# Feed-forward loop in fp32: paired bn_stats, half of the tanh additions on VectorE, gn and the statistics one step sooner

## The reference, cut to what matters

```python
def step(h, _):
    h = h + 0.01 * jnp.tanh(h)
    h = h * jax.nn.sigmoid(h)
    h = _layernorm(h, ln_w, ln_b)          # mean and variance over 64 features, eps 1e-5
    h = jnp.einsum('bsc,dc->bsd', h, W) + b
    return (h, None)
x, _ = jax.lax.scan(step, x, None, length=N_ITERS)    # N_ITERS = 30
...
h = h + _L0_ffn_ref(_layernorm(h, axis=-1), ...)      # 64 x 96 rows of 64 features
```

## Time and profile before

| what | us |
|---|---|
| runs shown | 2052.88, 2053.17, 2066.5 |
| median | 2053.17 |
| profiled execution, its own time | 2048.48 |
| its span | 2046.7 |
| TensorE, VectorE, ScalarE, GpSimd busy in the span | 1798.6, 1523.3, 1233.2, 861.9 |

### The profile page before, as it was taken

The page is one execution under the profiler, slowest core; times in us unless marked ns, Lnnn a source line. Parts: engine busy times, 40 slices in busy tenths (PEclk is TensorE's granted clock), DMA queues, the critical chain, the costliest instruction groups (busy, mean ns, idle before and its releaser), DMA issues. The chain is left out here.

```text
span 2046.7 us, 73424 instructions
## 1 busy us (share of the span) xinstructions
PE 1798.6 (88%) x25670; PEld 1546.0 (76%) x25701; DVE 1523.3 (74%) x4623; ACT 1233.2 (60%) x2911; POOL 861.9 (42%) x841
## 2 busy tenths in 40 slices
PE   2401299999999999999999999999958899999998
PEld 2401299999999999999999999999948477777776
DVE  3201188888888888888888888888857888888887
ACT  0100277777777777777777777777715466666665
POOL 5000123233332323232332323232214899999997
PEclk9999999999999999999999999999979899999999
DMA  3332200000000000000000000000022000000000
GB/s 116 75 74 60 61 18 19 17 19 17 19 17 17 19 17 19 17 19 17 19 17 17 18 17 19 17 19 17 13 57 62 1 0 0 0 0 0 0 0 31
DMA packets 60784, 48.85 MB, mean 24 GB/s; under 512 B 18368, under 2 KB 58108, under 8 KB 59772
## 3 DMA queue, kind: packets, MB, share of 16 engines
q1 hardware_dynamic: 58790, 47.72, 8.7%
q10 hardware_dynamic: 1972, 0.86, 0.2%
HBM read 19.92 MB, written 8.93 MB: 14 GB/s over the span
## 5 line engine op out<-in xcount | busy, mean ns | idle before, releaser
L681 POOL TENSOR_TENSOR y0lo<-y_whole,y0hi 125x384 f16<-125x384 f32 x410 | 376.2, 918 | 1048.0 <-ACT y_whole L639 1048.0
L643 ACT ACTIVATE z1hi<-ps 128x375 f16<-128x375 f32 x820 | 398.5, 486 | 341.2 <-PE ps L582 341.2
L706 DVE TENSOR_TENSOR z1lo<-ps,z1hi 128x375 f16<-128x375 f32 x820 | 449.8, 549 | 192.3 <-ACT z1hi L643 192.3
L581 PE MATMUL ps<-ATlo,y0hi 125*128 125x150 f16 x2460 | 584.6, 238 | 0.0
L580 PE MATMUL ps<-AThi,y0hi 125*128 125x150 f16 x2460 | 566.6, 241 | 2.0 <-POOL y0lo L681 2.0
L582 PE MATMUL ps<-AThi,y0lo 125*128 125x150 f16 x2460 | 564.5, 239 | 0.0
L711 DVE TENSOR_TENSOR y<-ps,negb 125x384 f32<-125x384 f32 x820 | 451.1, 550 | 29.6 <-PE ps L597 0.7
L595 PE MATMUL ps<-W1hi,z1hi 128*128 128x128 f16 x2460 | 459.3, 221 | 0.2 <-DVE y L711 0.2
L597 PE MATMUL ps<-W1hi,z1lo 128*128 128x128 f16 x2460 | 453.5, 219 | 0.0
L596 PE MATMUL ps<-W1lo,z1hi 128*128 128x128 f16 x2460 | 453.2, 219 | 0.0
L635 ACT ACTIVATE y0hi<-ps 125x384 f16<-125x384 f32 x820 | 404.8, 494 | 77.2 <-PE ps L560 77.2
(11 more groups left out here) (197 smaller groups left out, 2360.4 us busy)
## 6 DMA issues: line engine op xcount, KB each, us to landing
z_static<-zk SPq DMA_DIRECT2D x205, 93.8 KB, 1.9
pooled_rows<-stage SPq DMA_DIRECT2D x820, 2.5 KB
zk<-z_parts SPq DMA_DIRECT2D x16, 360.4 KB
xs<-in_x_v SPq DMA_DIRECT2D x3, 1201.2 KB
xs<-in_x_v SPq DMA_DIRECT2D x5, 720.7 KB
z_parts<-zp SPq DMA_DIRECT2D x20, 180.2 KB
parts<-pooled_rows SPq DMA_DIRECT2D x8, 256.0 KB, 6.1
h_rows<-h SPq DMA_DIRECT2D x16, 96.0 KB, 1.8
```

Of the source, the lines that this page charges most:

```text
L581: nc.tensor.matmul(o, hi, alo, start=False, stop=False, skip_group_check=True)
L643: nc.scalar.activation(z1hi[:, q, 0:GV], ps[:, Z1B + q % 2, 0:GV], ACT.Identity).then_inc(z1hi_done, 1)
L681: nc.gpsimd.tensor_tensor(y0lo[0:R, par, q, :], y0f[0:R, q, :], y0hi[0:R, par, q, :], ALU.subtract).then_inc(y0lo_by_pool, 1)
L706: nc.vector.tensor_tensor(z1lo[:, q, 0:GV], ps[:, Z1B + q % 2, 0:GV], z1hi[:, q, 0:GV], ALU.subtract).then_inc(z1lo_done, 1)
```

## The change

- **Statistics.** A bn_stats now reads two rows of 64 in alternation (`rearrange("p i d -> p d i")`): its even elements are one row, its odd elements the other. So its two triples are the whole statistics of two rows, and four bn_stats of 128 elements serve a chunk. `dm`, `s`, `q`, `sm` and the addition on GpSimd go; one `tensor_scalar` (L1338, 128x8) adds 64 eps to the squared parts and writes `var`. GpSimd keeps the power alone. In the first iteration the centring takes the mean straight from the pair (L1349).
- **Tanh addition.** Even chunks keep the matmul. For odd chunks VectorE does it in PSUM with one scalar_tensor_tensor (L1366), behind a wait for `th`. `y_ready` becomes two semaphores, one for each kind.
- **Order.** Lags: statistics and pow 2 to 1, gn 4 to 3, T 4 to 3; gT stays at 4 and the weights at 5. TensorE issues the addition ahead of the transposes; VectorE issues the odd addition first in its body.

```diff
         bs, bs0 = (sb(f"bn_pairs{i}", [P, 2, CP, 6]) for i in range(2))
...
                 def body(s, c, on, half):
-                    if on(2):
-                        n, b = s - 2, c % 2
-                        pool.wait_ge(parts_done, 2 * n + 2)
+                    if on(1):
+                        n, b = s - 1, (c - 1) % 2
+                        pool.wait_ge(var_done, n + 1)
                         if late(n, 2):
                             pool.wait_ge(gn_done, n - 1)
-                        inverse_roots(s2, q2, var, rs, b, n, var_done, rs_done)
+                        nc.gpsimd.tensor_tensor(rs[:, b, :], var[:, b, :], expo[:], ALU.pow).then_inc(rs_done, 1)
...
+                    if on(0) and c % 2 == 0:
+                        pe.wait_ge(th_done, s + 1)
+                        nc.tensor.matmul(ps[:, c, :], pct[:], th[:, c % 2, :], start=False, stop=True,
+                                         skip_group_check=True).then_inc(y_ready[0], 1)
-                    if on(4):
-                        n, b = s - 4, c % 2
+                    if on(3):
+                        n, b = s - 3, (c - 3) % 2
                         pe.wait_ge(gn_done, n + 1)
...
+                def statistics(src, pairs, var, b, n, bns, made):
+
+                    for j in range(CP):
+                        last = v_.bn_stats(pairs[:, b, j, :], src[:, 2 * j:2 * j + 2, :].rearrange("p i d -> p d i"))
+                    last.then_inc(bns, 1)
                     dve.wait_ge(bns, n + 1)
...
+                    v_.tensor_scalar(var[:, b, :], squares(pairs, b), D * EPS, None, ALU.add).then_inc(made, 1)
...
+                def body(s, c, on, half):
+                    if on(0) and c % 2 == 1:
+                        dve.wait_ge(th_done, s + 1)
+                        v_.scalar_tensor_tensor(ps[:, c, :], th[:, c % 2, :], 0.01, ps[:, c, :],
+                                                ALU.mult, ALU.add).then_inc(y_ready[1], 1)
+                    if on(3):
+                        n, cn, b = s - 3, (c - 3) % CH, (c - 3) % 2
                         dve.wait_ge(rs_done, n + 1)
```

More of the change, by code:

```diff
@@ L1196, in feed_forward @@
         gT = sb("gT", [P, 2, CP * P])
[L1198 to L1203, removed]
+        bs, bs0 = (sb(f"bn_pairs{i}", [P, 2, CP, 6]) for i in range(2))
         var, var0 = (sb(f"var64_{i}", [P, 2, CR]) for i in range(2))
@@ L1237, in steps, with squares, means @@
                     before(s)
-                body(s, s, lambda lag, s=s: s - lag >= 0)
+                body(s, s, lambda lag, s=s: s - lag >= 0, lambda lag, s=s: (s - lag) // 2)
             with eng.Fori(1, ITERS) as it:
                 for c in range(CH):
-                    body(it * CH + c, c, lambda lag: True)
+                    body(it * CH + c, c, lambda lag: True, lambda lag, c=c: it * (CH // 2) + (c - lag) // 2)
             for s in range(N, N + LAG):
-                body(s, s - N, lambda lag, s=s: 0 <= s - lag < N)
+                body(s, s - N, lambda lag, s=s: 0 <= s - lag < N, lambda lag, s=s: (s - lag) // 2)
         def late(n, k):
             return not isinstance(n, int) or n >= k
+        def squares(pairs, b):
+            return pairs[:, b].rearrange("p j (i k) -> p (j i) k", i=2)[:, :, 2]
+        def means(pairs, b):
+            return pairs[:, b].rearrange("p j (i k) -> p (j i) k", i=2)[:, :, 1]
         out_rows = out.rearrange("b s d -> (b s d)").rearrange("(c p n) -> c p n", c=CH, p=P)
@@ L1262, in _ @@
                 pool.wait_ge(expo_made, 1)
[L1264 to L1268, removed]
                 def first(c):
                     if c < CH:
[L1272 removed]
+                        pool.wait_ge(var0_done, c + 1)
                         if c >= 2:
                             pool.wait_ge(x0_ready, c - 1)
[L1275 removed]
+                        nc.gpsimd.tensor_tensor(rs0[:, c % 2, :], var0[:, c % 2, :], expo[:], ALU.pow).then_inc(rs0_done, 1)
                 first(0)
[L1278 to L1281 removed]
+                def body(s, c, on, half):
+                    if on(1):
+                        n, b = s - 1, (c - 1) % 2
+                        pool.wait_ge(var_done, n + 1)
                         if late(n, 2):
                             pool.wait_ge(gn_done, n - 1)
[L1284 removed]
+                        nc.gpsimd.tensor_tensor(rs[:, b, :], var[:, b, :], expo[:], ALU.pow).then_inc(rs_done, 1)
                 steps(pool, body, lambda s: first(s + 1))
@@ L1290, in _, with body @@
                 nc.scalar.activation(warm[:], ident[:, 0:1], ACT.Silu)
-                def body(s, c, on):
+                def body(s, c, on, half):
                     if on(0):
@@ L1295, in body @@
                         if late(s, 2):
-                            act.wait_ge(y_ready, s - 1)
+                            act.wait_ge(y_ready[c % 2], half(2) + 1)
                         nc.scalar.activation(th[:, c % 2, :], ps[:, c, :], ACT.Tanh).then_inc(th_done, 1)
@@ L1299, in body @@
                         n, cn = s - 1, (c - 1) % CH
-                        act.wait_ge(y_ready, n + 1)
+                        act.wait_ge(y_ready[cn % 2], half(1) + 1)
                         if late(n, NG):
@@ L1337, in body @@
                         last.then_inc(gT_ready, 1)
[L1338 to L1341, removed]
                 steps(pe, body, first)
@@ L1357, in centre @@
                 def centre(c):
                     b = c % 2
+                    rows = h2[:, c, :].rearrange("p (r d) -> p r d", d=D)
                     dve.wait_ge(h2_loaded, (c + 1) * 16)
                     if c >= 2:
[L1362 to L1371, removed]
+                        dve.wait_ge(rs0_done, c - 1)
@@ L1373, in first @@
+                        dve.wait_ge(centred, c - 1)
+                    statistics(rows, bs0, var0, b, c, bn0, var0_done)
+                    v_.tensor_tensor(x0c[:, b, :].rearrange("p (r d) -> p r d", d=D), rows,
+                                     spread(means(bs0, b), P, CR), ALU.subtract).then_inc(centred, 1)
                 def first(c):
@@ L1382, in _, with body @@
                 centre(0)
-                def body(s, c, on):
-                    if on(4):
-                        n, cn, b = s - 4, (c - 4) % CH, c % 2
+                def body(s, c, on, half):
+                    if on(0) and c % 2 == 1:
[4 more added lines that the diff above has]
+                        n, cn, b = s - 3, (c - 3) % CH, (c - 3) % 2
                         dve.wait_ge(rs_done, n + 1)
@@ L1391, in body @@
                                          spread(rs[:, b, :], P, CR), ALU.mult).then_inc(gn_done, 1)
-                    if on(2):
-                        n, cn, b = s - 2, (c - 2) % CH, c % 2
+                    if on(1):
+                        n, cn, b = s - 1, (c - 1) % CH, (c - 1) % 2
                         dve.wait_ge(g_done, n + 1)
                         if late(n, 2):
[L1396 to L1404, removed]
+                            dve.wait_ge(rs_done, n - 1)
+                        statistics(g_[:, cn % NG], bs, var, b, n, bn_done, var_done)
                 steps(dve, body, first)
```

14 lines of the change are left out of this document (1 added, 13 removed).

## The result

The changed kernel takes 1985.32 us (median of four runs, 1983.93 to 1991.66), the kernel before 2055.54 us (median of its four). The ratio is 0.9655, with a 95% interval of 0.9613 to 0.9697: 3.5% faster. The forecast was 2053 us, no change against the 2053.17 us of the runs it had; what came true is the rival of the free strides, with 1979 us.

What follows compares the result with a forecast made beforehand. TensorE bound the last stage at 4.81 us a pair of steps; VectorE would bind at 4.86: 87 pairs +4 us, tail -3, first chunks -1, in all about 0, so 2053 us, range 1975 to 2080.

Steps and rivals of the forecast that it cites:

- the rival of the free strides: Last stage: alternating bn_stats reads cost nothing extra, four take 0.86 us, a pair of steps 4.00; 1979 us, chance 0.27.
- the price of the alternating read: VectorE statistics: four bn_stats of 128 elements alternating between two rows take 1.32 us, ends 0.86 and 1.40.
- The limit moves to VectorE and stays at the same height: Last stage: VectorE needs 4.86 us a pair of steps, against TensorE's 3.96 and the old 4.81; chance 0.45.
- bn_stats at 0.28 us (free strides, step 2.0): Profile sign in the last stage that the forecast is wrong: each bn_stats 0.28 us, a step 2.0 us.
- the longest strided read there is: L888, 64 elements at 24 bytes: 260 ns against 222 contiguous, taken as the price for strided bn_stats.
- TensorE's pair: TensorE's work in two steps of the last stage falls from 4.81 to 3.96 us, every second addition gone.
- The addition in PSUM: VectorE's tanh addition, one a pair of steps: 0.60 us from start to start, bounds 0.59 and 0.75.
- The ring through gT: Old order: transposes, gT on ScalarE, L1327, next transposes hold a step at 2.41 us; the new order opens it.
- the drain: Last five steps, without additions: 12 us become a chain of 8.0 us, of which 3 us taken as gain.
- GpSimd: pow: Rival in the last stage: pow on GpSimd takes about 2.2 us, up to 4.5 a pair; 2022 us, chance 0.10 with half-priced strides.
- Taking out the addition alone would thus bring nothing: Last stage, old order: without the addition on TensorE the ring still holds the step at 2.41 us.
- The first chunks: First six chunks of the last stage lose sm, s and q and pay for strided reads: -1 us.

Runs made afterwards that it cites:

- experiment 6: The changed kernel with 48 more VectorE operations at the very end, six each of eight access patterns; one run, 1997.64 us.
- experiment 1: The kernel before with only the paired statistics of the change, old order and all tanh additions on TensorE; 2053.03 us, ratio 0.9982.
- experiment 2: Paired statistics and new order against the kernel before, all tanh additions still matmuls on TensorE; 2060.35 us, ratio 1.0019.
- experiment 3: Paired statistics and every second addition on VectorE against the kernel before, with the old order; 2127.6 us, ratio 1.0344.

## Why the prediction was wrong where it was wrong

**The step that failed** is the price of the alternating read: "I take 1.32 with 0.86 and 1.40 as ends." It measured 0.88, at the cheap end. So "The limit moves to VectorE and stays at the same height", to which 0.45 was given, did not happen: the limit stayed on TensorE and fell. This one term is more than the whole miss: put 0.88 into the forecast's own sum and VectorE needs 2.22 + 2 x 0.88 = 3.98 us a pair, TensorE 3.96, and the rival's line "87 x (4.00 - 4.81) = -70" follows; measured were -71.6 us up to the last step with an addition. (VectorE's measured sum is 3.82: 0.10 + 0.10 had been charged behind the bn_stats, and 0.03 + 0.09 was measured.) The prediction's own sign of being wrong, "bn_stats at 0.28 us (free strides, step 2.0)", is what the profile shows, with 283 ns and 1.985 us.

That 1985.32 us lies between 1975 and 2080 us is no merit of the forecast. The range had been stretched to take in the free strides, which had a chance of 0.27; the cause that it names for 2053 us was not at work.

I carried over a price from L888, because it was "the longest strided read there is". The number was real (experiment 6 repeats it: 266 ns against 219). What was wrong was to call the two patterns alike. The size was somewhat high too: at steps of 24 bytes bn_stats stood (1.79 - 0.37) / 5 = 0.284 us apart and took 0.370, so four would take 3 x 0.284 + 0.370 = 1.22 us, not 1.32. L888 steps by 24 bytes and comes to each place once; the new bn_stats goes forward in steps of 4 bytes along two rows at once.

The Trainium skill, in Advanced Engine Details and Errata, section SBUF Cachelines, says that a 16-byte line must be hit at least twice and that a different line at each access is penalised. On steps the runs agree: 8 bytes, two hits a line, 281 ns, and 16 bytes, one hit, 368. By its last clause the alternation should pay as well, and there the measurement decides against it for two rows (281 ns) and for it with four (359). That two rows are free because two lines are kept at hand is how I read this; no run shows the lines themselves.

**What was right.** TensorE's pair fell to 3.94 in the chain (3.96 worked out). The loop bound of both engines is close together, as the rival had it. The addition in PSUM took 0.60 (0.60 taken), 697 ns long (about 0.69). The granted clock in the loop stayed at 1.00. The ring through gT was seen rightly: its waits are there in experiment 1 and gone in experiment 2, and the drain fell from 12.03 to 8.07 us. (The idle time of 0.93 us that was read from the earlier trace rows is that of the weight loads; the matmul side of TensorE was idle for 0.69 there.) Moving gn a step sooner cost nothing: its waits for rs are 1.4 us over 180 steps. GpSimd: pow takes 1.75 us on average, 3.5 for a pair, which is below 3.97, so it doesn't become the bound.

**What was only half right.** "Taking out the addition alone would thus bring nothing": in the old order, with the addition put on VectorE, it costs 3.4% (experiment 3), because that addition joins the very ring that I had described, by way of th and gn. I had looked at the ring on TensorE and ScalarE and not at what stands behind a new wait in VectorE's queue.

**What was missed.** The first chunks. I took "-1" for them, for their statistics only; experiment 1 bears out the sign, with -2.8 (23.8 us where 26.65). But the new order, in which a wait for g stands ahead of the next x, adds 9.7 (experiment 2, 33.5), and the odd addition 2.7: 36.2, +9.6 net. The drain had been put at "3 us as gain"; it measured 4.0, and 3.7 in experiment 2.

**The parts need each other.** Statistics alone 0.998, statistics with the order 1.002, statistics with half of the additions 1.034, order with half of the additions 1.013, all three 0.966. Each pair leaves one of three limits standing: TensorE's 4.81, the ring, which with the addition in it takes 5.56 us a pair, or VectorE's 5.00.

## What to carry to other kernels

When the sign of a forecast hangs on one access pattern, don't take the price from the strided row that happens to be in the trace: ask first whether it is the same pattern in the terms that matter (how far each access goes, how many rows are walked at once, how often each is come back to). When a step is moved earlier in a queue, read the first pass through the loop on its own: a lag that is harmless in the steady state put a wait ahead of the work that feeds TensorE, and it cost 10 us, which came back, and more, by preparing two chunks ahead. And a change that removes one of several limits at the same height is worth nothing until the last of them is gone, so its parts can't be judged one by one.

## What the runs showed of the hardware that was not expected

- bn_stats of 128 fp32 elements on VectorE: 280 ns contiguous, 281 alternating between two rows 256 bytes apart, 281 at 8-byte steps, 356 to 374 at steps of 16 to 256 bytes and with four rows (128 bytes apart) or eight (256 bytes apart) in alternation.
- A tensor_tensor of 64 elements pays nearly as much for one input at 24-byte steps (257 ns) as for two (266), against 219.
- A scalar_tensor_tensor that reads and writes PSUM takes 697 ns for 128x512 and 0.60 us from start to start, the same as gn from SBUF to SBUF (688 ns, 0.61).
- In the first chunks the granted clock stayed at 0.50 (1.2 GHz) over the 20 us from 1600 to 1620 us, in which TensorE was busy for 4.15 and 5.27 of 10 us; with two chunks prepared ahead (7.29 and 7.69 of 10 us) it was 0.88 and 0.83. With five ahead it was 0.50 from 1600 to 1610 us with TensorE busy for 5.74 us, and 1.00 from 1610 to 1620 with 5.67. The copy of a chunk took 2.07 us at 0.50 and 1.13 at 1.00, so a low clock makes the ring of the beginning longer.
